# Eight products of probabilities and values in one double step of a head pair, where four stood in each of two

## The reference, cut to what matters

```python
# kind 1: keys and values come from a latent of width 64
kv_latent = x @ Wkv_down.T
scores = einsum('bqhd,bkhd->bhqk', q, k) * HEAD_DIM ** -0.5
out = einsum('bhqk,bkhd->bqhd', softmax(scores), v).reshape(b, t, 512) @ Wo.T
# kind 2: values are mixed from 5 experts per head, and outputs go through chosen experts
scores = einsum('bhid,bhjd->bhij', q * scale, k)
attn = einsum('bhij,bhjd->bihd', softmax(scores), v)
out = einsum('bthe,bthk,ekd->btd', mask_o, attn, Wo)
```

## The kernel before, in words

| slot C3 of the odd double step | where | count |
|---|---|---|
| queries, copied by ACT | run 0 d3; run 2 d1; runs 3, 5, ... 13 d1 and d7; run 15 d1 | 15 |
| experts or `absorb_out`, copied by ACT | runs 3, 5, ... 13 d5; run 1 d7; run 14 d7; run 0 d5 | 9 |
| transposes or `product_out2`, copied by DVE | run 1 d5; run 2 d3; runs 3, 5, ... 13 d3; runs 4, 6, ... 12 d1 and d3; run 14 d1, d3, d5 | 21 |
| nothing | run 0 d7; run 1 d1, d3; runs 2, 4, ... 12 d5 and d7; run 15 d3 | 16 |
| end of the last run | run 15 d5, d7 | 2 |

## Time and profile before

### The profile page before, as it was taken

How to read it: one execution, slowest core, us unless ns; L and a number is a source line. 1 busy time by engine, 2 the same in 40 slices (tenths; PEclk the granted TensorE clock), 3 DMA queues, 4 the chain that set the end, 5 groups by cost and what they waited for, 6 DMA issues and landing times. The chain is left out here.

```text
span 2805.2 us, 31491 instructions
## 1 busy us (share of the span) xinstructions
PE 2355.3 (84%) x10169; PEld 1157.3 (41%) x10169; DVE 1890.3 (67%) x3133; ACT 1673.2 (60%) x2352; POOL 1894.3 (68%) x1890
## 2 busy tenths in 40 slices
PE   5667777787777777775999899999999999999985
PEld 3222323232333323223555455555555555555542
DVE  5788989898888988763333356555656565666645
ACT  1778888879888888980122255554555555555440
POOL 5545577787878787873677303958585858595867
PEclk8668787878778787787899899999999999999997
DMA  3000000000000010114898400000010001000000
GB/s 104 16 1 1 18 16 16 18 16 18 9 25 8 10 23 3 24 20 110 228 272 212 111 1 1 1 1 23 1 23 1 23 1 23 1 8 1 9 1 16
DMA packets 91428, 98.97 MB, mean 35 GB/s; under 512 B 19296, under 2 KB 87008, under 8 KB 91232
## 3 DMA queue, kind: packets, MB, share of 16 engines
q1 hardware_dynamic: 66544, 69.80, 8.8%
q0 software_dynamic: 24688, 26.88, 4.9%
HBM read 69.98 MB, written 26.66 MB: 34 GB/s over the span
## 5 line engine op out<-in xcount | busy, mean ns | idle before, releaser
L1038 POOL TENSOR_TENSOR TT<-TT,SS 128x512 f32<-128x512 f32 x512 | 652.2, 1309 | 225.4 <-ACT SS L967 224.9
L1774 ACT ACTIVATE PR<-S,NM 128x512 f32<-128x512 f32 x512 | 345.3, 686 | 260.9 <-DVE NM L1941 260.9
L1941 DVE TENSOR_REDUCE NM<-S 128x2 f32<-128x1024 f32 x256 | 301.6, 1220 | 131.4 <-PE S L1668 131.4
L727 DVE TENSOR_SCALAR TT<-SC 128x1024 f32<-128x1024 f32 x256 | 311.6, 1217 | 76.8 <-POOL TT L1038 45.3
L457 PE MATMUL OB<-TT,VAL 128*17 128x512 f32 x1024 | 339.7, 766 | 7.9 <-ACT TT L975 7.9
L729 DVE SCALAR_TENSOR_TENSOR SS<-SC,TT 128x1024 f32<-128x1024 f32 x256 | 313.6, 1225 | 20.6 <-issue 1.8
L1043 POOL DMA_INDIRECT slot_tokens<-TID,IDX x224 | 228.0, 1018 | 101.0 <-issue 67.8
L1679 PE MATMUL TP<-ident,PR 128*128 128x128 f32 x2048 | 275.4, 278 | 16.0 <-DVE TT L1946 12.9
L1946 DVE COPY TT<-TP 128x512 f32<-128x512 f32 x256 | 176.3, 689 | 156.0 <-PE TP L1679 153.4
L1679 PEld LDWEIGHTS TP<-ident,PR 128*128 128x128 f32 x2048 | 234.1, 142 | 113.4 <-issue 75.3
L1780 ACT ACTIVATE TT<-TP 128x512 f32<-128x512 f32 x256 | 153.3, 599 | 197.4 <-PE TP L1679 193.6
(11 more groups left out here) (293 smaller groups left out, 4105.1 us busy)
## 6 DMA issues: line engine op xcount, KB each, us to landing
TT<-w_gu SPq DMA_DIRECT2D x64, 384.0 KB, 3.8
TT<-w_dn SPq DMA_DIRECT2D x64, 128.0 KB, 4.0
XL<-x SPq DMA_DIRECT2D x8, 512.0 KB, 4.0
rows<-XL SPq DMA_DIRECT2D x8, 512.0 KB, 8.4
TT<-w_dn SPq DMA_DIRECT2D x64, 64.0 KB, 4.7
XS<-stream SPq DMA_DIRECT2D x8, 512.0 KB, 4.2
out<-XS SPq DMA_DIRECT2D x8, 512.0 KB, 2.9
X<-x SPq DMA_DIRECT2D x7, 512.0 KB, 3.9
```

The costliest lines, as they stand in the source:

```text
L727: dve.tensor_scalar(tt[:, :, mt, :], SC[mt % 2][:], 0.0, None, ALU.max)
L1038: ins = pool.tensor_tensor(tt, tt, ss, ALU.add)
L1774: act.activation(PR[s % 2][h2][:], S[s % 2][:, h2, :], ACT.Exp, bias=NM[:, s % 2, h2:h2 + 1], accum_out=SM[:, pair % 2, j, h2:h2 + 1]).the ...
L1941: dve.tensor_reduce(NM[:, s % 2, :], S[s % 2][:], AX, ALU.max, negate=True).then_inc(sems["peak"], 1)
```

## The change

`attend` for the head pair that ended runs for all four key tiles in the even double step (s % NT == 0) and not at all in the odd one. Before, key tiles 0 and 1 ran in the even double step, 2 and 3 in the odd one. Nothing else is edited; the last head pair of the last run has its own loop, which stays.

```diff
                 rr, pair = behind(r, s)
-                if rr >= 0:
-                    attend(v, rr, pair, s % NT, False)
-                    attend(v, rr, pair, s % NT + 1, False)
+                if rr >= 0 and s % NT == 0:
+                    for m in range(NT):
+                        attend(v, rr, pair, m, False)
                 carry(v, parts, r, d, 3, 4)
```

## The result

| | before | after |
|---|---|---|
| median (4 runs each, taken together) | 2829.85 (2828.05 to 2830.84) | 2903.94 (2901.74 to 2910.69) |
| the profiled execution | 2806.97 | 2901.74 |
| its span | 2805.2 | 2900.0 |
| first scores of stage three | 1588.86 | 1611.96 |
| stage three, from there to the end | 1216.34 | 1288.04 |

The kernel became slower by 74.1 us: the ratio of the times is 1.0273 (1.0255 to 1.029). The prediction said 2917, a loss of 88.

The account below looks back on a forecast made before the run. PE was taken to bound the kernel's middle. Losses of 25.4 + 18.3 + 31.5 + 16.8 us, less 3.7 swallowed by long waits, made 88.3; added to the median 2828.87 this gave 2917, range 2880 to 2950.

Parts of the forecast that it names:

- 1.87 us each: Even double steps: the added products delay all that follows, with no PE wait to swallow it, costing 1.87 us each.
- four cases: Odd double steps by slot C3: nothing loses 1.59 us, queries 1.22, DVE's copies 1.50, experts 1.87 per pair of double steps.
- The long waits: Two even double steps wait 5.29 and 5.65 us for POOL and DVE, swallowing the 1.87 us added there: -3.7 us.
- counted at nothing: Last two odd double steps: PE waits for POOL's mixed values anyway, so no loss; uncovered, 3 to 4 us.
- Rival 1: Odd double steps: only the probabilities hold PE up, never BK; loss 48 us, time 2877, chance 0.11.
- Rival 2: Gaps in odd double steps also lower PE's clock: 34 us on top of the forecast, 2951, chance 0.12.
- Rivals 3 and 4: No measurable change, PE's work being merely reordered: 2829, chance 0.04; or faster by 8 us: 2821, chance 0.03.
- rival 4: DVE's `set_down` stops waiting 0.37 us for products in 21 double steps: 8 us faster, 2821, chance 0.03.

Follow-up runs that it names:

- e2_three_one: Against the kernel before: three key tiles in the even double step, one in the odd one; 2847.72 us, ratio 1.0061.
- run 14: Not a follow-up: a numbered stretch of double steps in stage three of every kernel, behind the middle; its d6 holds a wait of 5.65 us before.
- e3_copies_first: The changed kernel, but in odd double steps ACT and DVE make slot C3's copy earlier; 2870.71 us, ratio 1.0148 to the kernel before.
- e6_join_two: The kernel before, 11 pairs with out2 in even slot C3 joined in odd double steps, DVE's odd slot C3 copies early; 2830.57 us, ratio 1.0003.
- run 9: Not a follow-up: a numbered stretch of double steps in the middle of stage three of every kernel; a middle pair of such takes 141.98 us before.
- e4_join_free: The kernel before, 19 head pairs with output products in even slot C3 given all four key tiles in the odd double step; 2827.61 us, ratio 0.9991.

## Why the prediction was right, and where its sum was off

**The mechanism held.** PE sets the time in the middle, and the products with values are the cover of the chain from scores to probabilities and to the copies of BK. Taken from the odd double step, they leave waits there; put into the even one, they are added in full. Marks, forecast and measured in after:

| | forecast | measured |
|---|---|---|
| turn with nothing in slot C3 | t + 3.27 | t + 3.36 |
| next item there | t + 4.43 | t + 4.49 |
| item behind queries | t + 5.83 | t + 5.76 |
| item behind DVE's copies | t + 4.87 | t + 4.78 |
| item behind experts | t + 5.84 | t + 5.83 |

The start of the stage, with no products at all, was thus a good picture of the turns and of the items behind queries in the odd double steps to come.

**The term that was too large** is "1.87 us each" of the even double steps. Four key tiles in one group take 3.58, so what was added there is 1.72. Of the four cases this leaves, per double step of the middle, 1.40 to 1.50 lost with nothing in slot C3 (forecast 1.59), 1.02 with queries (1.22), 1.08 to 1.26 with DVE's copies (1.50) and 1.72 with experts (1.87). Much of each difference is the 0.15. The rest is what the odd double steps gave back: 0.46 to 0.54 behind DVE's copies where 0.37 was forecast, 0.70 behind queries where 0.65 was, 0.22 or 0.32 with nothing in slot C3 where 0.28 was. The sum by parts of stage three, in the profiled executions:

| | forecast | measured |
|---|---|---|
| up to the end of run 3 | 21.1 | 12.0 |
| runs 4 to 13, five pairs | 5 x 12.0 = 60.0 | 50.4 |
| runs 14 and 15 | 7.3 | 9.2 |
| sum | 88.4 | 71.7 |

61 groups at 0.15 make 9.2 of the 16.7 us between them. Forty of them lie in the second row (6.0 us of its 9.6); most of the rest there are the differences just named, and d2 of kind 1, which grew by 1.61 and not by 1.72. In the first row the long wait of run 3 is the greater part. The third row holds 5.9 us that are no wait at all, as said below.

**The long waits.** This is the step of the working that failed. The prediction let each of the two swallow 1.87 us, which is what is added in its own double step. That of run 3 d2 (5.29 us) is gone altogether: the rows above have no wait, and the double step is 5.35 us shorter although its products take 1.72 us more. So 7.1 us went where 1.87 was counted, 5.2 more. POOL's work on XN, for which PE waits there, in before and in after, then PE's wait in e2_three_one, then the stretch behind the wait in before (columns of the earlier trace rows):

```profile
1827.62 4.82 POOL L2017 TENSOR_SCALAR XN<-XS,mvl,rstd1b 128x256 f32<-128x256 f32 x4 [0.17 <-issue]
...
1860.12 4.83 POOL L2017 TENSOR_SCALAR XN<-XS,mvl,rstd1b 128x256 f32<-128x256 f32 x4 [0.17 <-issue]
...
1856.79 1.09 PE L1503 MATMUL BK<-ident,XN 128*128 128x128 f32 x4 [2.77 <-POOL XN L2017]
...
1831.52:1838.34 6.82, 5.75 (x22) 4.43 (x24) 1.43 (x3) 1.20 (x2) 6.51 (x6) 0.50 0.01 2
```

Counted from the stage's start, POOL is done 9.4 us later in after (1864.95 - 1611.96 against 1832.44 - 1588.86), and PE comes there 17.9 us later: 16.2 lost ahead of this double step and 1.72 in it. The difference, 8.5 us, is more than the whole wait. In e2_three_one PE comes 3.9 us later and POOL is done 1.4 later, and 2.77 of the 5.29 us are left. So a wait for an engine off the path swallows what PE has lost ahead of it in the pipeline, less what that engine was held up itself, and not only what is added in its own double step. The wait makes some 5.5 of the 7.1 us. The other 1.6 are the clock: behind the wait it was at 0.50 in before, and the first transposes there took 1.09 us where they take 0.60 in after. The wait of run 14 d6 stayed, 3.9 of 5.65 us, as the prediction had it.

The last run, counted at nothing for its last two head pairs, lost 3.2 us from d4 on. POOL's mixed values cover the start of that stretch, which gained 2.7 (d4 and d5). The 5.9 lost behind it are the clock, and no wait. The last output products (L1628) in before, after, e3_copies_first and e6_join_two:

```profile
2794.60:2801.41 6.81, 6.81 (x24) 3.88 (x24) 1.26 (x3) 0.00 (x0) 0.00 (x0) 1.00 0.00 0
...
2883.50:2896.18 12.68, 12.68 (x24) 6.69 (x24) 1.26 (x3) 0.00 (x0) 0.00 (x0) 0.50 0.00 0
...
2854.13:2860.95 6.82, 6.82 (x24) 3.89 (x24) 1.26 (x3) 0.00 (x0) 0.00 (x0) 1.00 0.00 0
...
2817.95:2830.64 12.69, 12.69 (x24) 6.70 (x24) 1.26 (x3) 0.00 (x0) 0.00 (x0) 0.50 0.00 0
```

The same 24 instructions take 6.8 us at 1.00 and 12.7 at 0.50. This does not follow the place of the products: e3_copies_first has them as in after and ran at 1.00, e6_join_two has those of the last run as in before and ran at 0.50. No term of the sum stands for it. Without it runs 14 and 15 lost 3.3 us (9.2 - 5.9) where 7.3 were forecast, and the stage 65.8 (71.7 - 5.9) where 88 were. So it is in part luck that the profiled stage comes as near to the forecast as it does; how the other executions ended is not on record.

**The rivals.** Rival 1, that only the probabilities hold PE up, falls with the waits for ACT's copies (L1743, L1762) in after, and with e3_copies_first, where moving the copies alone took 3.3 us out of the pair. Rival 2, that the clock falls too, falls for the middle: 1.00 over 948.91 us, with PE busy 889.05 of them and a pause of 0.8 to 1.4 us in most odd double steps. Outside of it the clock did fall, in before too. Two of the falls in after came behind pauses of 0.35 to 1.37 us, at 1687.44 and at 1803.49; the fall that ends the middle came behind one of 3.93:

```profile
1803.49:1806.90 3.41, 3.41 (x15) 2.51 (x15) 1.38 (x2) 0.60 (x1) 3.07 (x5) 0.50 0.00 0
...
2755.67 1.88 PE L1679 MATMUL TP<-ident,PR 128*128 128x128 f32 x8 [3.93 <-DVE TT L1946]
...
2755.81:2759.22 3.41, 3.41 (x12) 2.54 (x11) 0.69 (x1) 0.60 (x1) 0.00 (x0) 0.50 0.00 0
```

The two early ones cost 1.3 and 1.6 us against e3_copies_first, which has the same pauses just ahead of these places and stayed at 1.00. Before has falls that after lacks, which cost it 1.2 us at the earlier trace rows and 2.7 behind the wait of run 3, so that the clock leaves little in the first row of the sum. By the rule of the Trainium skill that was weighed there (TensorE: Matmul & The Clock Gate, section "A second HAM failure mode: psum-queue depth-cycling") the clock should have swung between its levels; here pauses of this length brought two such falls at most, and none in the middle. Rivals 3 and 4, no change and faster, fall with the times. What rival 4 rests on is real, `set_down` waits no more; but the even double steps hid nothing.

## What to carry to other kernels

Where one engine is busy all the time, its work is also the cover of the other engines' chains: before work of that engine is gathered in one place, measure the chain that it leaves bare (here scores, maximum, exponentials and copy, 3.2 to 5.8 us) at a place of the trace where the cover is missing anyway, such as the pipeline's start. The price of the move is then the time that is added at the one place less the time that the other can really give back, case by case. Gathering itself is worth little (0.15 us for a group here), and where it costs nothing on the busy engine, it can still move a short instruction of another engine further into a long one of a third.

## What the runs showed of the hardware that was not expected

- A group of products with values costs 0.857 us per key tile and 0.15 us once: 1.01, 1.87, 2.73 and 3.58 us for one to four key tiles. Inside a group the pairs of products start 0.43 us apart; behind the first pair it is 0.48 and behind the last 0.53 (runs before and after). So the 0.15 falls at the change from and to products of other tiles, and is saved when two groups are joined.
- An instruction of DVE on 128 x 4 numbers that takes 0.17 us at its shortest took 1.24, 1.59 and 1.69 us (run 9 d1 of before, e4_join_free and e6_join_two) beside an addition of POOL on 128 x 1280 that runs 2.9 us, and ended with it. In the eight traces it lasted over 0.2 us in 60 of 128 places, and in all 60 it ended 0.02 to 0.03 us behind an instruction of POOL. The Trainium skill, SBUF — State Buffer, section "SBUF: two separate sides", tells of a pair of ports which DVE and GpSimd hold by turns for a whole instruction, while the other waits. These rows agree with it; that POOL's addition is the cause was not tried by itself.
- PE's granted clock stayed at 1.00 through 48 pauses of 0.8 to 1.4 us and one of 2.2 in 948.91 us, and was at 0.50 for 3.41 us behind the one of 3.93. Twice in the early runs of after it fell behind pauses of 0.35 to 1.37 us, where e3_copies_first, with the same pauses just ahead, kept 1.00.
